# Gate and up product of a routed feed-forward: expert weights made the stationary operand, transposes of the activation left out

## The reference, cut to what matters

```python
logits = x @ router_weight.T + router_bias
top_val, top_idx = jax.lax.top_k(logits, 4)
top_val = jax.nn.softmax(top_val, axis=-1)
gate_up = jnp.einsum('th,ehd->etd', x, gate_up_proj) + gate_up_proj_bias[:, None, :]
gate, up = gate_up[..., ::2], gate_up[..., 1::2]
gate = jnp.minimum(gate, LIMIT)
up = jnp.clip(up, -LIMIT, LIMIT)
glu = gate * jax.nn.sigmoid(gate * ALPHA)
out = jnp.einsum('etd,edh->eth', (up + 1.0) * glu, down_proj) + down_proj_bias[:, None, :]
out = (out * router_scores.T[:, :, None]).sum(axis=0)
```

## Time and profile before

| what | value |
|---|---|
| median of three runs | 796.6 us (795.14 to 798.18) |
| the profiled execution's own time | 802.32 us |
| its span | 800.5 us |
| PE busy | 635.2 us (79%) |
| PE weight loads | 408.9 us (51%) |
| DVE busy | 537.2 us (67%) |
| ACT busy | 458.7 us (57%) |
| POOL busy | 396.1 us (49%) |

### The profile page before, as it was taken

The page is one execution under the profiler, slowest core; times in us unless marked ns, Lnnn a source line. Parts: engine busy times, 40 slices in busy tenths (PEclk is TensorE's granted clock), DMA queues, the critical chain, the costliest instruction groups (busy, mean ns, idle before and its releaser), DMA issues.

```text
span 800.5 us, 13282 instructions
## 1 busy us (share of the span) xinstructions
PE 635.2 (79%) x3658; PEld 408.9 (51%) x3658; DVE 537.2 (67%) x1570; ACT 458.7 (57%) x933; POOL 396.1 (49%) x300
## 2 busy tenths in 40 slices
PE   5887979598998752302999999999999999997450
PEld 2344636264565541201666666666666666664230
DVE  3637487778878978500777777777777777771892
ACT  2777686547546533101666767767767767762242
POOL 0012214654845737752466666666666656565121
PEclk9979798889989856555999999999999999997555
DMA  7966754799522223253677777776777676645987
GB/s 250 423 238 106 150 92 71 224 318 347 158 86 101 89 72 119 106 207 99 112 114 110 111 113 111 108 114 109 113 113 114 108 114 102 108 58 76 350 149 102
DMA packets 111895, 115.35 MB, mean 144 GB/s; under 512 B 31730, under 2 KB 101506, under 8 KB 110162
## 3 DMA queue, kind: packets, MB, share of 16 engines
q0 software_dynamic: 35456, 50.35, 37.2%
q1 hardware_dynamic: 76370, 64.16, 26.7%
HBM read 55.15 MB, written 59.31 MB: 143 GB/s over the span
## 4 chain that ended last, share of the span: by engine, by line
PE 59%; DVE 12%; DMA 8%; POOL 7%; ACT 6%; issue 5%; SPq 2%; POOLq 0%; ACTq 0%; DVEq 0%
PE PS L633 8%; PE PS L634 8%; PE PS L635 8%; PE PS L502 7%; POOL routed L916 6%; PE PS L624 4%; PE PS L653 4%; PE PS L641 4%; PE PS L654 4%; PE PS L655 4%; PE PS L525 2%; PE PS L533 2%; DMA W<-w_dn 2%; DMA W<-neg_mem 1%; DVE small L1325 1%
## 5 line engine op out<-in xcount | busy, mean ns | idle before, releaser
L942 POOL DMA_INDIRECT sums<-arena x144 | 223.2, 1550 | 143.8 <-ACT arena L702 71.5
L916 POOL DMA_INDIRECT routed<-arena,small x128 | 142.7, 1115 | 90.6 <-DVE small L1162 45.3
L1303 DVE TENSOR_SCALAR arena<-PS,small 128x256 f32<-128x256 f32 x144 | 78.3, 544 | 126.7 <-ACT arena L875 124.7
L702 ACT ACTIVATE arena<-PS 128x512 f16<-128x512 f16 (+1 forms) x180 | 105.1, 589 | 78.7 <-PE PS L624 45.7
L502 PE MATMUL PS<-arena 128*128 128x512 f32 x256 | 134.0, 668 | 10.7 <-ACT arena L702 10.6
L875 ACT ACTIVATE arena<-PS,small 128x256 f32<-128x256 f32 x144 | 68.1, 473 | 104.1 <-PE PS L635 104.1
L633 PE MATMUL PS<-W,arena 128*128 x288 | 110.2, 382 | 0.0
L634 PE MATMUL PS<-W,arena 128*128 x288 | 110.1, 382 | 0.0
L635 PE MATMUL PS<-W,arena 128*128 x288 | 109.9, 382 | 0.0
L502 PEld LDWEIGHTS PS<-arena 128*128 128x128 f32 x256 | 51.9, 214 | 69.3 <-issue 65.8
L624 PE MATMUL PS<-ident,arena 128*128 128x128 f16 x576 | 56.3, 221 | 36.7 <-DMA arena<-routed 35.9
(11 more groups left out here) (164 smaller groups left out, 1023.3 us busy)
## 6 DMA issues: line engine op xcount, KB each, us to landing
arena<-routed SPq DMA_DIRECT2D x144, 128.0 KB
W<-w_gu SPq DMA_DIRECT2D x8, 1024.0 KB, 23.6
W<-neg_mem POOLq DMA_DIRECT2D x16, 512.0 KB, 8.5
sums<-zero SPq DMA_DIRECT2D x2, 4096.0 KB, 26.2
W<-sums SPq DMA_DIRECT2D x16, 512.0 KB, 8.8
X<-x SPq DMA_DIRECT2D x8, 512.0 KB, 4.8
W<-w_dn SPq DMA_DIRECT2D x4, 1024.0 KB, 11.4
out<-X SPq DMA_DIRECT2D x8, 512.0 KB, 3.0
```

Of the source, the lines that this page charges most:

```text
L702: return nc.scalar.activation(o, i, ACT.Copy, **kw)
L916: pool.indirect_dma_start(routed, bass.IndirectOffsetOnAxis(ap=idx, axis=0), rows[b][:, jk // TOPK, :], None).then_inc(rows_sent[lane], 16)
L942: pool.indirect_dma_start(sums[j % SUMS], bass.IndirectOffsetOnAxis(ap=dst[j % MU], axis=0), yb[u], None, compute_op=ALU.add).then_inc(y_s ...
L1303: L.send(v.tensor_scalar(up[j % 2], acc[:, FF:2 * FF], gu_hi, gu_lo, ALU.min, ALU.max))
```

## The change

`gate_up` exchanges the operands. The expert's weights become the stationary operand, in blocks of 128x128, and the 128 tokens of the tile the moving one. The result has the hidden numbers on the partitions: columns 0 to 255 of the bank are the two blocks of the gate, 256 to 511 those of up. That is the layout that `down` wants, so the activation is no longer transposed: `act_transposes`, `aT_mm` and its PSUM banks go away, and both halves are made straight from `act_` in SBUF. The lags become 2 and 3. The freed bank gives `xT16` a second buffer. Two waits are new: `gate_up` of PE waits for `act_ready` of tile j - 3, whose bank it overwrites (before, the transposes' wait covered that), and ACT's copy to `ah` waits for `y2_mm` of tile t - 2, which frees the buffer.

```diff
-A_LAG, D_LAG = 3, 4
+A_LAG, D_LAG = 2, 3
...
-        xT16 = PS[:, 3, 0:DIM].bitcast(f16)
+        xT16 = [PS[:, 3 + b, 0:DIM].bitcast(f16) for b in range(2)]
...
             def row_transposes(j):
                 pe.wait_ge(x_in[j % UN], 16 * (j // UN + 1))
-                if j >= 1:
-                    pe.wait_ge(xq_ready, j)
+                if j >= 2:
+                    pe.wait_ge(xq_ready, j - 1)
...
             def gate_up(j, e):
                 acc = PS[:, j % 3, :]
                 pe.wait_ge(xq_ready, j + 1)
+                if j >= 3:
+                    pe.wait_ge(act_ready, j - 2)
                 w = W16[:, ds(e * (2 * PART) + GU0 * 2 * PART, 2 * PART)]
-                for k in range(KT):
-                    hi, lo = [w[:, h * PART + k * 2 * FF:h * PART + (k + 1) * 2 * FF] for h in range(2)]
-                    mm(acc, xq[j % NX][:, k, :], hi, start=(k == 0), stop=False)
-                    mm(acc, xq[j % NX][:, k, :], lo, start=False, stop=False)
-                    last = mm(acc, xq[j % NX][:, KT + k, :], hi, start=False, stop=(k == KT - 1))
+                for f in range(2 * FF // P):
+                    part = acc[:, f * P:(f + 1) * P]
+                    for k in range(KT):
+                        hi, lo = [w[:, h * PART + k * 2 * FF + f * P:h * PART + k * 2 * FF + (f + 1) * P] for h in range(2)]
+                        mm(part, hi, xq[j % NX][:, k, :], start=(k == 0), stop=False)
+                        mm(part, hi, xq[j % NX][:, KT + k, :], start=False, stop=False)
+                        last = mm(part, lo, xq[j % NX][:, k, :], start=False, stop=(k == KT - 1))
                 last.then_inc(gu_mm, 1)
-
-            def act_transposes(j):
-                pe.wait_ge(act_ready, j + 1)
-                for k in range(KT):
-                    last = nc.tensor.transpose(PS[:, 4 + j % 2, k * P:(k + 1) * P],
-                                               act_[j % NB][:, k * P:(k + 1) * P], ident)
-                last.then_inc(aT_mm, 1)
...
                 if 0 <= j - A_LAG < TILES:
                     t = j - A_LAG
-                    act.wait_ge(aT_mm, t + 1)
-                    copy(ah[t % 2], PS[:, 4 + t % 2, 0:FF].rearrange("p (k t) -> p k t", k=KT),
+                    if t >= 2:
+                        act.wait_ge(y2_mm, t - 1)
+                    act.wait_ge(act_ready, t + 1)
+                    copy(ah[t % 2], act_[t % NB].rearrange("p (k t) -> p k t", k=KT),
                          scale=act_scale).then_inc(ah_ready, 1)
...
             def a_low(j):
                 dve.wait_ge(ah_ready, j + 1)
-                v.scalar_tensor_tensor(al[j % 2], PS[:, 4 + j % 2, 0:FF].rearrange("p (k t) -> p k t", k=KT),
+                v.scalar_tensor_tensor(al[j % 2], act_[j % NB].rearrange("p (k t) -> p k t", k=KT),
                                        act_scale, ah[j % 2], ALU.mult, ALU.subtract).then_inc(al_ready, 1)
```

More of the change, by code:

```diff
@@ L214, in build @@
         meta = [cut(2) for _ in range(MU)]
-        identY = cut(P)
-        xT16 = PS[:, 3, 0:DIM].bitcast(f16)
+        xT16 = [PS[:, 3 + b, 0:DIM].bitcast(f16) for b in range(2)]
         ah, al = [[cut(DIM // 2).bitcast(f16).rearrange("p (k t) -> p k t", k=KT) for _ in range(2)]
@@ L314, in build @@
         meta_in = [sem(f"meta_in{u}") for u in range(MU)]
-        identY_ready = sem("identY_ready")
         gu_mm = sem("gu_mm")
         sg_ready, act_ready = sem("sg_ready"), sem("act_ready")
-        aT_mm, ah_ready, al_ready, y2_mm = sem("aT_mm"), sem("ah_ready"), sem("al_ready"), sem("y2_mm")
+        ah_ready, al_ready, y2_mm = sem("ah_ready"), sem("al_ready"), sem("y2_mm")
         y2_ready = sem("y2_ready")
@@ L620, in row_transposes @@
                 pe.wait_ge(x_in[j % UN], 16 * (j // UN + 1))
-                if j >= 1:
-                    pe.wait_ge(xq_ready, j)
+                if j >= 2:
+                    pe.wait_ge(xq_ready, j - 1)
                 for k in range(2 * KT):
-                    last = nc.tensor.transpose(xT16[:, k * P:(k + 1) * P], xrow[j % UN][:, k * P:(k + 1) * P], ident16[:, :])
+                    last = nc.tensor.transpose(xT16[j % 2][:, k * P:(k + 1) * P], xrow[j % UN][:, k * P:(k + 1) * P], ident16[:, :])
                 last.then_inc(x_mm, 1)
@@ L660, in tile_step @@
                     row_transposes(j + 1)
-                if 0 <= j - A_LAG < TILES:
-                    act_transposes(j - A_LAG)
                 if j >= D_LAG:
@@ L854, in evac_row @@
                     act.wait_ge(gu_mm, j + 1 - NX)
-                copy(xq[j % NX].rearrange("p k t -> p (k t)"), xT16).then_inc(xq_ready, 1)
+                copy(xq[j % NX].rearrange("p k t -> p (k t)"), xT16[j % 2]).then_inc(xq_ready, 1)
             def tile_step(j):
```

## The result

| | before | after |
|---|---|---|
| median | 797.39 us (795.14 to 800.53, four runs) | 885.05 us (884.38 to 886.32, four runs) |
| the profiled execution | 802.32 us | 886.32 us |
| its span | 800.5 us | 884.5 us |
| PE busy | 635.2 us (79%) | 721.7 us (82%) |

The account below looks back on a forecast made before the run. The prediction took PE's full array, tied with the ACT/DVE chain at 2.40 us, as the bound, and its sequencer as the next: 140 × (3.04 − 2.40) = +90, less 4, on the 796.6 median gives 883 us, range 848 to 915.

Parts of the forecast that it names:

- the two terms of that sum, loop and tail: Whole run: 140 steps × (3.04 − 2.40) = +90 us in the tile loop, less 4 at the end, +86.
- The array work, 2.21 us: PE array, per step: 24 matmuls at 0.055 take 1.33 against 1.29, activation's transposes go (−0.23): 2.40 becomes 2.21 us.
- the rival built on loads: gate_up on PE: loads of 128 columns don't overlap, step 3.23 us, 909 us (about 852 by the skill's figure); chance 0.04.
- The sequencer work, 3.04 us: PE's sequencer, per step: 20 register instructions × 0.13 + 3 semaphore instructions × 0.12 + 0.08 = 3.04 us, bounds 2.87 to 3.21.
- The 0.13 us for a register instruction: PE's sequencer: cost of each of 20 address instructions in a tile, bounds 0.123 and 0.137 us.
- The 0.08 a tile for the expert numbers: PE's sequencer: the read of twelve expert numbers, 0.9 us spread over twelve tiles, hidden before and then paid in full.
- threes, 0.25 to 0.26 us apart: Sign inside gate_up: weight loads come in threes at that distance if the sequencer is the limit.
- The 0.12 for a semaphore instruction: PE's sequencer: assumed cost of each of three semaphore instructions in a step, bounds 0.11 and 0.13 us.
- The chain through ACT and DVE: From gate_up through ACT and DVE to down: at most 2.8 us a step, covered by 3.04; 2.42 without the sequencer limit.
- The ends: After the loop: POOL's scatters no longer fall behind, taking back 4 us of 6 (bounds 0 and 6).
- The rival that had it fall to half: PE's clock in the tile loop drops to 0.50, 4.3 us a tile; half the loop there gives 970 us; chance 0.07.
- The rival that ended faster: Tile loop: register instruction under 0.09 us and two chain steps under 4.42, so the array's 2.21 sets 770 us; chance 0.04.

Follow-up runs that it names:

- plain_scatters: fixed_experts_three with POOL's scatters writing in place of adding, against the kernel before: 0.959 (0.954 to 0.964), 767.4 us against 799.1.
- fixed_experts: The changed kernel with the expert of gate_up's weights fixed in the program, 16 register instructions a tile fewer; against the kernel before 0.995, 810.2 us against 810.7.
- addresses_ahead: The changed kernel with all addresses of down and gate_up worked out in one block between row transposes and down; against the kernel before 1.067 (1.058 to 1.076).
- own_address_after: The changed kernel with the second of each three gate_up matmuls working out its own address, 8 register instructions more a tile; 1.300 against the kernel before.
- fixed_experts_three: fixed_experts with a third buffer for ah and al and D_LAG 4; against the kernel before 1.004 (1.000 to 1.008).

## Why the prediction was right

883 us were predicted and 885.05 measured; the difference of the medians is 87.7 us where the sum had 86. In the profiled executions the two terms of that sum, loop and tail, come to 93.6 − 5.6 = 88.0.

- **The array work, 2.21 us.** Right: plain_scatters runs at 2.22. The doubt was whether loads and matmuls of 128 columns keep 0.055 us in a long row. They do, at 0.056 over 24 of them (fixed_experts and addresses_ahead). The Trainium skill's 81 ns for a sustained stream of such pairs (page "TensorE: Matmul & The Clock Gate", section "Back-to-back issue gap") isn't what these runs show, and the rival built on loads is refuted by fixed_experts.
- **The sequencer work, 3.04 us.** Right in mechanism and size: 3.06 over 136 tiles against 3.04. That sum holds 0.08 for the expert numbers, so for an ordinary step it says 2.96, and the ordinary steps measure 2.98 on average; the one shown, at 3.04, is among the longer ones. The 0.13 us for a register instruction is 0.134 by own_address_after. The 0.08 a tile for the expert numbers is 0.9 us each twelfth tile in the row of waits. The "threes, 0.25 to 0.26 us apart" are there in most of the loads shown, with a longer gap now and then. The 0.12 for a semaphore instruction was not measured by itself.
- **The chain through ACT and DVE.** Covered, as predicted: DVE is at 57.5% and ACT at 56.7% against 58 and 55 foretold. That it would hold 2.42 if the sequencer didn't limit is borne out by fixed_experts (2.41), and by fixed_experts_three, which loosens it and reaches 2.23 for a while.
- **The ends.** 5.6 us came back where I took 4, inside the bounds. The loop's 93.6 against 90 is mostly the 0.02 us more per step, 2.8 us over 140 steps.
- **The clock.** The rival that had it fall to half is refuted for this kernel: 1.00 at 73% of array work. Even in own_address_after, 2.21 of work in 4.13 us, it is 0.98.
- **The rival that ended faster.** It named two conditions, a cheap register instruction and a short chain. The runs showed that a third was missing. With the sequencer and the chain both out of the way, fixed_experts_three is at 1.004 and not at the 0.966 that 770 us would be; only with POOL's adding scatters replaced is it 0.959. This didn't touch the forecast, but the row stood in the profile of before: POOL's last scatter 6.4 us behind the last copy. I used it for the ends, and didn't ask what step it would allow.

## What to carry to other kernels

Count the instructions that an engine's sequencer executes per unit of work, not only those that show as busy: cutting one matmul whose address is computed at run time into four multiplies the address work, which costs nothing while the array's own work covers it and is paid in full above that. If such addresses must be many, spread them a stage ahead in small groups; one block of them is hidden only as far as the queue ahead of the array reaches, about 1 us here. And before crediting an engine's shorter step, ask each other loop of the pipeline for its own pace: here the array (2.40 us a tile before the change), the chain (2.42) and the adding scatters (2.4 to 2.5) lay side by side.

## What the runs showed of the hardware that was not expected

- The sequencer's lead over the array at the end of a `gate_up` was about 18 matmuls of 128 columns with their loads, some 1.0 us, in addresses_ahead and also in plain_scatters, where the sequencer has time to spare.
- An instruction with six register operations is shown with 74 ns and one with three with 46, but from start to start they take 0.13 (560.9 to 562.1 for ten) and 0.123: joining operations pays.
- ACT's copy to `ah` takes 506 ns from SBUF, and took 476 from PSUM; DVE's `a_low` takes 480 and took 479. Moving a source from PSUM to SBUF saved nothing. After the change, and then before it (400 to 740 us):

```profile
L695 ACT ACTIVATE arena<-arena,small 128x256 f16<-128x256 f32 x144 | 72.8, 506 | 0.6 <-DVE arena L1300 0.6
```

```profile
L702 ACT ACTIVATE arena<-PS,small 128x256 f16<-128x256 f32 x137 | 65.2, 476 | 0.0
```
